# A graph step with an expert layer on one core: equality masks stored in the order in which TensorE reads them

## The reference

```python
# edge part
H = layernorm(x).astype(f16); v = edge_weight.astype(f16)
msgs = H[dst] * v[:, None]
x = x + segment_sum(msgs, src, num_segments=50000)
# expert part, on h = layernorm(x)
probs = softmax(h @ gate_w + gate_b); idx = argmax(probs)
pos = place of the token in its expert's queue; kept = pos < C
y = relu(h @ w1[idx] + b1[idx]) @ w2[idx] + b2[idx]
x = x + nan_to_num(y * prob * kept)
```

## Time and profile before

| | us |
|---|---|
| median of three runs | 3526.37 |
| lowest, highest run | 3525.03, 3540.87 |
| profiled execution | 3569.06 |
| its span | 3567.3 |
| busy in it: PE / weight loads | 2846.6 / 2603.9 |
| busy in it: DVE / ACT / POOL | 2245.0 / 1539.7 / 1724.4 |

### The profile page before, as it was taken

The page is one execution under the profiler, slowest core; times in us unless marked ns, Lnnn a source line. Parts: engine busy times, 40 slices in busy tenths (PEclk is TensorE's granted clock), DMA queues, the critical chain, the costliest instruction groups (busy, mean ns, idle before and its releaser), DMA issues.

```text
span 3567.3 us, 60077 instructions
## 1 busy us (share of the span) xinstructions
PE 2846.6 (80%) x18806; PEld 2603.9 (73%) x18807; DVE 2245.0 (63%) x5836; ACT 1539.7 (43%) x2638; POOL 1724.4 (48%) x1183
## 2 busy tenths in 40 slices
PE   4553434067677777499999999999999999999998
PEld 3443433067676667399898999888999989998987
DVE  5645555076566566377666677676677776667666
ACT  2322222044444444255444555454455545554443
POOL 4788887635555566333434333343433343334323
PEclk8666666555555555699999999999999999999999
DMA  8544444388787776311211211121211121111111
GB/s 313 153 89 77 87 78 86 29 269 252 249 259 248 228 240 207 115 48 56 66 57 44 72 48 52 49 67 57 67 48 47 56 67 47 48 51 49 42 47 37
DMA packets 306007, 374.74 MB, mean 105 GB/s; under 512 B 34887, under 2 KB 266340, under 8 KB 302608
## 3 DMA queue, kind: packets, MB, share of 16 engines
q1 hardware_dynamic: 224608, 202.49, 19.3%
q0 software_dynamic: 77728, 145.22, 14.9%
q10 hardware_dynamic: 3600, 26.22, 1.8%
HBM read 185.42 MB, written 196.46 MB: 107 GB/s over the span
## 4 chain that ended last, share of the span: by engine, by line
PE 53%; DVE 4%; issue 1%; DVEq 0%; DMA 0%; SPq 0%; ACT 0%; POOL 0%; POOLq 0%; ACTq 0%
PE u_Y L1181 27%; PE u_H L1170 23%; PE u_T L1153 3%; DVE y L1110 1%; DVE yo L1129 1%; DVE yo L1126 1%; DVE y L1115 0%; DVE hn L1078 0%; DVE low L1120 0%; DVE hlo L1098 0%; DVE yo L1124 0%; DMA slots<-blank 0%; DMA u_pay<-slots 0%; DVE scales L1073 0%; DVEq L1078 0%
## 5 line engine op out<-in xcount | busy, mean ns | idle before, releaser
L1010 POOL DMA_INDIRECT out_x<-yo,u_token x348 | 668.5, 1921 | 1261.4 <-DVE yo L1131 1179.5
L1181 PE MATMUL u_Y<-whi,hhi 128*128 128x256 f32 x2784 | 784.2, 282 | 1.5 <-DVE hlo L1098 1.5
L1181 PE MATMUL u_Y<-wlo,hhi 128*128 128x256 f32 x2784 | 775.4, 279 | 0.0
L1181 PE MATMUL u_Y<-whi,hlo 128*128 128x256 f32 x2784 | 774.8, 278 | 0.0
L1046 ACT ACTIVATE hm<-u_H,b1e 128x512 f32<-128x512 f32 (+1 forms) x736 | 487.9, 663 | 639.8 <-PE u_H L1170 627.0
L539 POOL DMA_INDIRECT slots<-pay,slot_i x392 | 415.3, 1059 | 325.5 <-DVE slot_i L748 210.3
L1170 PE MATMUL u_H<-xhi,whi 128*128 128x512 f32 (+1 forms) x1472 | 563.6, 383 | 8.0 <-issue 5.5
L1170 PE MATMUL u_H<-xhi,wlo 128*128 128x512 f32 (+1 forms) x1472 | 562.2, 382 | 0.0
L1170 PE MATMUL u_H<-xlo,whi 128*128 128x512 f32 (+1 forms) x1472 | 560.2, 381 | 0.0
L1181 PEld LDWEIGHTS u_Y<-whi,hhi 128*128 128x128 f32 x2784 | 528.4, 190 | 1.7 <-DVE hlo L1098 1.7
L1181 PEld LDWEIGHTS u_Y<-wlo,hhi 128*128 128x128 f32 x2784 | 528.8, 190 | 0.0
(11 more groups left out here) (137 smaller groups left out, 3747.9 us busy)
## 6 DMA issues: line engine op xcount, KB each, us to landing
xt<-in_x SPq DMA_DIRECT2D x49, 1024.0 KB
out_x<-pay SPq DMA_DIRECT2D x49, 1024.0 KB
u_pay<-slots SPq DMA_DIRECT2D x93, 534.0 KB, 3.8
agg<-zeros ACTq DMA_DIRECT2D x25, 1024.0 KB
at<-agg SPq DMA_DIRECT2D x49, 512.0 KB
raw<-in_L_ffn_w POOLq DMA_DIRECT2D x14, 1024.0 KB
src_row<-in_src SPq DMA_DIRECT2D x25, 512.0 KB
slots<-blank SPq DMA_DIRECT2D x8, 801.0 KB, 5.1
```

Source lines behind the costliest of these rows:

```text
L1010: pool.indirect_dma_start(out=out[:, :], out_offset=bass.IndirectOffsetOnAxis(ap=token[:, s:s + 1], axis=0), in_=yo[:, s, :], in_offset=No ...
L1181: last = pe.matmul(ps_Y[:, s, 0:D], a[:, f, rows], w2_at(w, buf, f), start=(f == 0 and j == 0), stop=(f == KF - 1 and j == 2))
```

## The change

`same` keeps its size and gets the shape [partition, buffer, mask, column a, partition p]. Each mask is still one comparison of 1024 elements, but it reads `src_row` in the order a-major: 128 elements with a distance of eight int32 (32 bytes), eight times over, and writes 1024 contiguous f16. What `earlier` and TensorE read from a mask, the 128 elements of one column, is then one contiguous piece of 256 bytes, where it had been 128 elements 16 bytes apart. Values, number and order of all instructions, waits and DMAs are the same.

```diff
-    same = sb("same", [P, 2, G, STEP], F16)
+    same = sb("same", [P, 2, G, G, P], F16)
...
                 for c in chunks:
-                    last = v.tensor_scalar(same[:, h, c, :], src_row[:, q, :], srcf[:, h, c:c + 1], None,
-                                           ALU.is_equal)
+                    last = v.tensor_scalar(same[:, h, c], src_row[:, q, :].rearrange("j (p a) -> j a p", a=G),
+                                           srcf[:, h, c:c + 1], None, ALU.is_equal)
...
                 for c in range(G):
-                    last = v.tensor_tensor(earlier[:, h, c, :],
-                                           same[:, h, c, :].rearrange("j (p a) -> j a p", a=G)[:, c, :],
-                                           before[:], ALU.mult)
+                    last = v.tensor_tensor(earlier[:, h, c, :], same[:, h, c, c, :], before[:], ALU.mult)
...
-                seen = lambda b, c: same[:, h, b, :].rearrange("j (p a) -> j a p", a=G)[:, c, :]
+                seen = lambda b, c: same[:, h, b, c, :]
```

## The result

The changed kernel takes 3596.70 us (median of 4 runs, 3589.04 to 3606.98) against 3533.62 us of the kernel before in the same session (4 runs, 3525.03 to 3541.57): ratio 1.0181 [1.0135, 1.0226], **63 us slower**. The forecast was 3541 us, "same" the likeliest; 3596.70 lies 23 us above the upper end of its range.

What follows compares the result with a forecast made beforehand. POOL's issues were taken to bound the edge stage: +15 us from scatters under longer masks, +1 in the first 111 us, about -1 from `earlier`, so +15 us on 3526.37 gives 3541 us; range 3520 to 3574.

Steps and rivals of the forecast that it cites:

- What bounds the kernel: Edge stage, 111.3 to 604.6 us: POOL's gather and scatter issues are the bound, 26.0 us a step; DVE has 11.45 slack.
- A mask holds POOL until its end: POOL's issues beside DVE's masks: POOL gets through only at the boundary between two masks, 0.664 us apart before the change.
- T = 1.06: Distance in us between the starts of two successive masks on DVE, 0.664 before, forecast to become 1.06 through strided reads.
- the forecast's 79 ns: Estimated cost of the stride in an `earlier` product of 128 elements, 371 ns against 292 contiguous; 0.62 ns an element.
- `earlier` at 292 ns or less, worth nothing: DVE's `earlier` products: 371 ns falls to 292, 0.6 us a step or about 1.2 at doubled rate, inside DVE's slack.
- Weight loads worth nothing: TensorE's loads of `same` become contiguous; POOL does not wait for PE, so nothing is gained even at half length.
- The first 111 us, +1: Start of the edge stage, before POOL's first scatter: exposed longer masks cost +1 us, between -2 and +5.
- Further scatters under masks: each rounded up to a multiple of T: POOL's steady steps: a 1.85 us scatter becomes 2.12, +0.77 us a step, +15 us over twenty mask phases.
- The rival of long holds: Masks of 1.20 us or more hold POOL longer: +34 to +46 us, about 3566 us; chance 0.20.
- the strided row: The one earlier profile row with a strided read, the `earlier` products, from which the masks' surcharge was estimated.

Runs made afterwards that it cites:

- e7: Changed kernel, with one added strided cast a step into a buffer that masks read contiguously: 3539.91 us against 3532.87 of the kernel before, ratio 1.0022.
- e9: Kernel before, with contiguous masks lengthened from 1024 to 1538 elements by an unused tail: 3568.32 us against 3529.47, ratio 1.0124.
- e11: Kernel before, with contiguous masks lengthened from 1024 to 2248 elements by an unused tail: 3600.16 us against 3529.47, ratio 1.0194.
- e10: Kernel before, with contiguous masks lengthened from 1024 to 1938 elements by an unused tail: 3590.40 us against 3529.47, ratio 1.0182.
- e6: Changed kernel, with strided masks lengthened to 148 elements in place of 128 in each of eight pieces: 3598.26 us, ratio 1.0189 to the kernel before.
- e5: Kernel before, with contiguous masks lengthened from 1024 to 1766 elements by an unused tail: 3591.63 us against 3532.87, ratio 1.0180.
- e4: Kernel before, with each mask made by a two-source tensor_tensor comparison in place of tensor_scalar: 3524.76 us against 3440.45, ratio 1.0245.

## Why the prediction was wrong, step by step

- **What bounds the kernel**: right. All of the loss is in POOL's busy time, none in a wait for DVE or TensorE.
- **A mask holds POOL until its end**: right in the main. The two gathers of the first step moved from 24.40 and 25.73 to 24.35 and 26.44, from 1.33 to 2.09 us, again twice T. But the next gather there, from 28.54, took 4.34 us to the one after it, four masks.
- **T = 1.06**: right, 1.050. The stride's price was 0.386 us on a mask of 1024, between the 0.32 and the 0.48 taken from the `earlier` products. The way there is less sure than the number: contiguous products turned out at 218 ns, so it is open how much of the 153 ns that they gained was the stride, and the forecast's 79 ns were carried over to a one-source operation on int32, which no run of before had shown.
- **`earlier` at 292 ns or less, worth nothing**: it came to 218 ns. By the doubled rate that the prediction takes from the Trainium skill (VectorE: DVE Perf Modes, "The perf-mode tier table"), 1.2 us a step less, the estimate is about 225, so this was nearer than the contiguous rows of larger types. Worth nothing it was: DVE's wait for rows is 10.44 us in the step shown and 13.21 in the next (forecast about 9) where it was 11.45.
- **Weight loads worth nothing**: right; e7, with the masks' length held, shows no gain.
- **The first 111 us, +1**: right, 111.31 to 112.39, though the hit is partly luck: these are single executions, and e9, with longer masks than before, has its first scatter at 108.79. The last zero fill even went out sooner than in the earlier trace rows, at 102.02:

```profile
102.02 0.82 ACTq L250 DMA_DIRECT2D agg<-zeros  x2
```

- **"Further scatters under masks: each rounded up to a multiple of T"**: this step failed. It made a scatter 2.12 us at T = 1.06; the trace has 3.29 to 3.46. In the step shown, three scatters with an excess of 1.45, 1.44 and 1.61 us come to 4.5 us, where the forecast had 1.34. That is +3.36 us on the mean step in place of +0.77, and 19 x 3.36 = 64 us in place of 15. The rule had been drawn from one T, 0.664, where "1.85 rounded up" and "1.19 and 0.66, each rounded up" both give three masks. The gathers that the rule was drawn from follow it at both lengths, but for the one of 28.54. The earlier trace rows held a hint: the scatter of 326.58 has a length of 1.99 and so a distance of 2.3 us, which rounding 1.85 to 1.99 does not give.
- **The rival of long holds** had the sign, but not the mechanism: it needed a T of 1.20 or more, and T stayed at 1.050. At 1.300 it set +2.3 us a step and +46 in all; e11, with that T, has +3.0 a step (28.98 less 25.96) and +70.7 in all, so this case was priced too low as well.
- The range ended at the dearest T that the strided row allowed. The doubt was put into T, which was right, and none into the rounding rule, which carried every figure of the sum.

Still open: which two accesses a scatter makes; why some issues pass over a mask's end and wait for a later one, as the scatters of four masks in the kernel after; why DVE gives way at T = 0.590 and POOL at all other lengths; the mixed distances of e10, e6 and a part of e5; and the 12 to 17 us by which the strided kernels are dearer than contiguous ones of the same T.

## What to carry to other kernels

Where GpSimd issues indirect DMAs back to back and bounds a stage, the price of a DVE instruction beside it can be not its own time but the time for which it holds GpSimd's issues, in whole instructions: here 0.39 us more on each of eight masks, all within DVE's slack, cost POOL 3.4 us a step. Before carrying such a rounding rule to another length, measure it at two lengths; one length fits several rules, and even the better rule here misses a part of the scatters. What helped most was neither a shorter mask nor a contiguous one, but a source in PSUM: no scatter grew, although the masks are then nearly twice as long.

## What the runs showed that was not expected

- A scatter's issue of 1.85 us takes 2.02 to 2.10 us beside masks 0.396 apart, about 2.1 at 0.664, 2.9 at 0.931, 3.2 at 1.050 and only about 2.5 at 1.196: the cost is not monotonic in the length of DVE's instruction.
- A two-source DVE operation of 1.14 us in SBUF held one issue for 5.76 us (e4).
- A one-source operation on int32 read 32 bytes apart took 1.050 us from start to start for 1024 elements and 0.590 for 512, against 0.664 and 0.396 contiguous.
- A contiguous f16 product of 128 elements took 218 ns, against 371 with one operand 16 bytes apart; a weight load 104 to 115 ns against 151 to 162.
